# A graph layer with residual layer norm: GpSimd takes the first split of x, VectorE takes all the scaling, the first source columns are loaded directly, the short super is merged

## The reference

```python
x_i, x_j = x[dst], x[src]                       # x: 100000 x 48, f32
tmp = concatenate([x_i, x_j, edge_attr], 1)     # 25000 x 128
msg = relu(tmp @ W1 + b1) @ W2 + b2             # 25000 x 48
y = x + segment_sum(msg, dst, 100000)
out = (y - mean(y)) / sqrt(var(y) + 1e-5)       # per node, over 48 values
```

## Time and profile before

| | |
|---|---|
| runs | 394.97, 395.75, 395.84 us; median 395.75 |
| profiled execution | 395.34 us, its span 393.6 us |
| PE busy | 358.6 us, 91% |
| DVE busy | 369.7 us, 94% |
| ACT busy | 285.1 us, 72% |
| POOL busy | 281.6 us, 72% |
| gathers L877 | 196, mean 1084 ns |
| GpSimd's scales L886 | 72, mean 920 ns |
| queue q1 (SP) | 58.74 MB, 65.2% of 16 engines' span |

### The profile page before, as it was taken

One profiled execution on the slowest core, in us unless ns is written; L12 is line 12 of the kernel. 1 busy time (PEld: TensorE's weight loads), 2 busy tenths in 40 slices (PEclk: granted clock), 3 DMA queues, 4 the chain that ended last, 5 costly groups with the idle time before them and its releaser, 6 DMA issues.

```text
span 393.6 us, 18011 instructions
## 1 busy us (share of the span) xinstructions
PE 358.6 (91%) x6802; PEld 324.1 (82%) x6802; DVE 369.7 (94%) x1044; ACT 285.1 (72%) x791; POOL 281.6 (72%) x284
## 2 busy tenths in 40 slices
PE   3169999989999999999999999999999999999981
PEld 2047888878999999999998989998999999999971
DVE  6655999999999999999999999999999999999975
ACT  1046776776788787888787878878788878788861
POOL 6777777771688888888888888888888888212120
PEclk9999999999999999999999999999999999999995
DMA  4576889888878989989989989988988888753122
GB/s 87 103 152 129 134 182 212 182 180 206 181 160 178 185 180 183 198 181 201 206 166 231 200 173 198 218 186 177 231 181 176 199 191 164 174 152 98 49 81 78
DMA packets 165601, 66.38 MB, mean 169 GB/s; under 512 B 95213, under 2 KB 165554, under 8 KB 165554
## 3 DMA queue, kind: packets, MB, share of 16 engines
q1 hardware_dynamic: 152762, 58.74, 65.2%
q0 software_dynamic: 6272, 4.83, 9.7%
q10 hardware_dynamic: 6520, 2.26, 2.5%
HBM read 38.46 MB, written 27.33 MB: 167 GB/s over the span
## 4 chain that ended last, share of the span: by engine, by line
PE 66%; DVE 20%; POOL 4%; issue 4%; DMA 3%; ACTq 0%; SPq 0%; ACT 0%; DVEq 0%
PE bank L993 12%; PE bank L1013 11%; PE bank L1001 10%; PE bank L982 10%; PE bank L956 8%; PE bank L1020 8%; PE bank L950 6%; POOL rows L877 4%; DVE onehot L1262 3%; DVE sq_total L1280 3%; DVE ys L1238 3%; DVE total L1229 3%; DVE x_rest L1268 2%; DVE ys L1298 2%; DVE msg_rest L1245 1%
## 5 line engine op out<-in xcount | busy, mean ns | idle before, releaser
L877 POOL DMA_INDIRECT rows<-in_x_dram,src_cols x196 | 212.5, 1084 | 53.2 <-issue 50.4
L1082 ACT ACTIVATE onehot_t<-bank 128x384 bf16<-128x384 bf16 (+1 forms) x261 | 117.9, 491 | 18.4 <-PE bank L956 18.3
L1020 PEld LDWEIGHTS bank<-w,hid_t 128*128 128x128 f32 x522 | 95.5, 190 | 23.1
L886 POOL TENSOR_TENSOR ys<-ys,rstd 128x432 f32<-128x432 f32 x72 | 66.2, 920 | 46.3 <-DVE rstd L1288 45.2
L1020 PE MATMUL bank<-w,hid_t 128*128 128x48 f32 x522 | 82.5, 239 | 0.0
L956 PE MATMUL bank<-ident_b,onehot 128*128 128x128 bf16 (+1 forms) x782 | 73.1, 221 | 8.9 <-DVE onehot L1262 8.5
L1262 DVE TENSOR_SCALAR onehot<-node_of,cat 128x384 bf16<-128x384 f16 x260 | 69.0, 320 | 10.0 <-DMA cat<-edge_table 10.0
L1001 PE MATMUL bank<-cat_t,w 128*128 128x384 f32 (+1 forms) x176 | 71.3, 486 | 0.5 <-ACT cat_t L1070 0.5
L993 PE MATMUL bank<-msg,onehot 128*128 128x48 bf16 (+1 forms) x782 | 69.1, 184 | 2.2 <-DVE msg_low L1252 2.2
L1013 PEld LDWEIGHTS bank<-xs,onehot_t 128*128 128x128 bf16 (+1 forms) x782 | 69.2, 104 | 1.6 <-issue 0.9
L1013 PE MATMUL bank<-xs,onehot_t 128*128 128x48 bf16 (+1 forms) x782 | 69.6, 184 | 0.7 <-ACT onehot_t L1082 0.7
(11 more groups left out here) (109 smaller groups left out, 816.8 us busy)
## 6 DMA issues: line engine op xcount, KB each, us to landing
out_dram<-ys SPq DMA_DIRECT2D x43, 432.0 KB
xs<-in_x_dram SPq DMA_DIRECT2D x78, 216.0 KB
cat<-edge_table SPq DMA_DIRECT2D x261, 40.5 KB
edge_table<-rows SPq DMA_DIRECT2D x65, 121.5 KB
rows<-in_x_dram,src_cols POOLq DMA_INDIRECT x196
rows<-in_edge_attr_dram SPq DMA_DIRECT2D x28, 96.0 KB
xs<-in_x_dram ACTq DMA_DIRECT2D x8, 216.0 KB
rows<-in_edge_attr_dram ACTq DMA_DIRECT2D x1, 384.0 KB, 5.5
```

What stands on the lines that cost most here:

```text
L877: pool.indirect_dma_start(rows[:, t, 0:D], None, x[:, :], bass.IndirectOffsetOnAxis(ap=src_cols[:, t:t + 1], axis=0)).then_inc(xsrc_in[s], 16)
L886: pool.tensor_tensor(y, y, rstd[0:n, v, 0:m].unsqueeze(2).broadcast_to([n, m, D]), ALU.mult).then_inc(normed, 1)
L1020: last = pe.matmul(msg_ps[:, k * D:(k + 1) * D], hid_t[:, v % SMALL, k * P:(k + 1) * P], w2[:, :], start=False, stop=(k == blocks - 1))
L1082: act.activation(onehot_t[0:n, v % SMALL, k, 0:jj * P], onehot_ps[k % 2][0:n, 0:jj * P], ACT.Copy).then_inc(onehot_t_ready, 1)
```

## The change

GpSimd no longer scales. It makes x_rest for supers 10 on (RESTS_FIRST), in a loop that first issues the gathers for super g + 6, then waits for x of g and for the scale of super g - 6 (REST_BEHIND). VectorE makes x_rest for supers 0 to 9 and scales every super. Its list has another order: x_rest ahead of the message's split, the message's two splits next to each other, and x_low behind the onehots. The indices of the first three gathers are loaded as three columns of 128 by ScalarE's queue, ahead of its other loads. The 160 left nodes become the third block of super 86: 53 partitions of three nodes and one of one node. NS is 87, and the last super's x and output go in three transfers each. Its unused partitions hold what an earlier super left in the buffer.

```diff
-LEAD = 14
+LEAD = 6
+RESTS_FIRST = 10
+REST_BEHIND = 6
...
-FIRST_SCALED = 12
-LAST_SCALED = 4
+LAST_PARTS = 3
...
-    NS = FULL_SUPERS + 2
+    NS = NB // SUPER
...
         def wait_scaled(eng, g):
-            if FIRST_SCALED <= g < NS - LAST_SCALED:
-                eng.wait_ge(normed, g - FIRST_SCALED + 1)
-            else:
-                eng.wait_ge(dve_normed, g + 1 if g < FIRST_SCALED else g + 1 - (NS - LAST_SCALED - FIRST_SCALED))
+            eng.wait_ge(dve_normed, g + 1)
...
+        def last_rows(table, tile):
+            w, first, s = J * D, FULL * BLOCK, (NS - 1) % BODY
+            before, here = (SUPER - 1) * w, (NS - 1) * SUPER
+            return ((table[0:first, :].rearrange("(b p j) d -> p b (j d)", p=BP, j=J)[:, here:FULL, :],
+                     tile[:, s, 0:before].rearrange("p (b m) -> p b m", b=SUPER - 1)),
+                    (table[first:first + REST_P * J, :].rearrange("(p j) d -> p (j d)", j=J),
+                     tile[0:REST_P, s, before:before + w]),
+                    (table[first + REST_P * J:N, :].rearrange("(p j) d -> p (j d)", j=REST_J),
+                     tile[REST_P:REST_P + 1, s, before:before + REST_J * D]))
...
+                if g < NS - 1:
+                    sp.dma_start(sbuf_rows(xs, v), dram_rows(x, g)).then_inc(x_in[v], 16)
+                    return
+                for there, here in last_rows(x, xs):
+                    sp.dma_start(here, there).then_inc(x_in[v], 16)
...
+                if g == NS - 1:
+                    wait_scaled(sp, g)
+                    for there, here in last_rows(out, ys):
+                        sp.dma_start(there, here).then_inc(y_out[v // PAIR], 16)
+                elif g % PAIR == 0:
+                    wait_scaled(sp, g + PAIR - 1)
+                    sp.dma_start(dram_rows(out, g, PAIR), sbuf_rows(ys, v, PAIR)).then_inc(y_out[v // PAIR], 16)
...
+                if t == GROUP:
+                    pool.wait_ge(src_placed, 1)
+                cols = src_first if t < GROUP else src_cols
...
-            def scale(g):
-                n, blocks, jj = shape_of(g)
-                v, m = g % BODY, blocks * jj
-                pool.wait_ge(rstd_ready, g + 1)
-                y = by_node(ys, g, v)
-                pool.tensor_tensor(y, y, rstd[0:n, v, 0:m].unsqueeze(2).broadcast_to([n, m, D]),
-                                   ALU.mult).then_inc(normed, 1)
+            def less_high_x(g):
+                r, v = divmod(g, BODY)
+                pool.wait_ge(x_in[v], 16 * (r + (LAST_PARTS if g == NS - 1 else 1)))
+                pool.wait_ge(dve_normed, g - REST_BEHIND + 1)
+                pool.tensor_tensor(x_rest[:, v, :], xs[:, v, :], upper_half(xs[:, v, :]),
+                                   ALU.subtract).then_inc(pool_x_rest_ready, 1)
...
-            pool.wait_ge(src_placed, 1)
+            pool.wait_ge(src_first_in, 16 * GROUP)
...
-            for g in range(FIRST_SCALED, NS):
+            for g in range(RESTS_FIRST, NS):
                 for gathered in range(gathered, tiles_for(g + LEAD)):
                     gather_xsrc(gathered)
                 gathered = tiles_for(g + LEAD)
...
-                if g < NS - LAST_SCALED:
-                    scale(g)
+                less_high_x(g)
...
         def _(act):
+            for t in range(GROUP):
+                act.dma_start(src_first[:, t:t + 1], src[t * P:(t + 1) * P].rearrange("(p a) -> p a", a=1)).then_inc(src_first_in, 16)
             load_ends(act, 0, src, src_in)
...
             def less_high_x(g, r, v):
-                dve.wait_ge(x_in[v], 16 * (r + 1))
+                if g >= RESTS_FIRST:
+                    return
+                dve.wait_ge(x_in[v], 16 * (r + (LAST_PARTS if g == NS - 1 else 1)))
...
             def less_middle_x(g, r, v):
-                dve.wait_ge(x_rest_ready, g + 1)
+                if g < RESTS_FIRST:
+                    dve.wait_ge(x_rest_ready, g + 1)
+                else:
+                    dve.wait_ge(pool_x_rest_ready, g - RESTS_FIRST + 1)
...
-            walk(dve, ((4, total_sum), (5, total_squares), (4, centre), (3, less_high_msg), (0, less_high_x), (3, less_middle_msg),
-                       (0, less_middle_x), (-1, make_onehot), (5, invert), (5, scale_some), (0, flag_general)), looped=False)
+            walk(dve, ((4, total_sum), (5, total_squares), (4, centre), (0, less_high_x), (3, less_high_msg), (3, less_middle_msg),
+                       (-1, make_onehot), (0, less_middle_x), (5, invert), (5, scale), (0, flag_general)), looped=False)
```

More of the change, by code:

```diff
@@ L415, in gnn_resnorm_kernel @@
     NB = FULL + 1
-    RJ = 2
-    RP = REST // RJ
-    assert RP * RJ == REST and RP <= P and 0 < FULL % SUPER
+    REST_P = REST // J
+    REST_J = REST - REST_P * J
+    assert NB % SUPER == 0 and 0 < REST_P < P and 0 < REST_J < J
     FULL_SUPERS = FULL // SUPER
-    NS = FULL_SUPERS + 2
+    NS = NB // SUPER
     ROUNDS = (FULL_SUPERS - 3) // BODY
@@ L425, in gnn_resnorm_kernel @@
     EREST = E - EP * EC
-    assert NS % PAIR == 0 and BODY % PAIR == 0
+    assert NS % PAIR == 1 and BODY % PAIR == 0
     assert EP == P - 1 and 0 < EREST < EC
@@ L560, in gnn_resnorm_kernel @@
         src_in = sem("src_in")
+        src_first_in = sem("src_first_in")
         next_shifted = sem("next_shifted")
@@ L670, in wait_scaled, with sbuf_rows @@
         def wait_scaled(eng, g):
-            if FIRST_SCALED <= g < NS - LAST_SCALED:
-                eng.wait_ge(normed, g - FIRST_SCALED + 1)
-            else:
-                eng.wait_ge(dve_normed, g + 1 if g < FIRST_SCALED else g + 1 - (NS - LAST_SCALED - FIRST_SCALED))
+            eng.wait_ge(dve_normed, g + 1)
         def dram_rows(table, g, supers=1):
-            n, blocks, jj = shape_of(g)
[L680 to L691, removed]
+            return table[0:FULL * BLOCK, :].rearrange("(b p j) d -> p b (j d)", p=BP, j=J)[:, g * SUPER:(g + supers) * SUPER, :]
+        def sbuf_rows(tile, s, supers=1):
+            return tile[:, s:s + supers, :].rearrange("p s (b m) -> p (s b) m", b=SUPER)
+        def last_rows(table, tile):
[7 more added lines that the diff above has]
+                     tile[REST_P:REST_P + 1, s, before:before + REST_J * D]))
         def rows_in(g, r):
@@ L812, in load_nodes @@
                     sp.wait_ge(sum_done, g - BODY + 1)
-                sp.dma_start(sbuf_rows(xs, g, v), dram_rows(x, g)).then_inc(x_in[v], 16)
-            def store(g):
[L817 to L822, removed]
+                if g < NS - 1:
[3 more added lines that the diff above has]
+                    sp.dma_start(here, there).then_inc(x_in[v], 16)
+            def store(g):
+                v = g % BODY
+                if g == NS - 1:
[5 more added lines that the diff above has]
+                    sp.dma_start(dram_rows(out, g, PAIR), sbuf_rows(ys, v, PAIR)).then_inc(y_out[v // PAIR], 16)
             def nodes_behind(g):
@@ L1261, in make_onehot @@
                 for k in range(blocks):
-                    last = dve.tensor_scalar(onehot[:, v, k, 0:n * jj], nodes[:, 0:n * jj], float((first_block(g) + k) * BLOCK),
+                    last = dve.tensor_scalar(onehot[:, v, k, 0:n * jj], node_of[:, :], float((first_block(g) + k) * BLOCK),
                                              cat[:, v, k, P:P + 1], ALU.add, ALU.is_equal)
```

38 lines of the change are left out of this document (14 added, 24 removed).

## The result

The changed kernel takes 405.29 us, median of three runs (404.81 to 406.36), against 395.75 us before: ratio 1.0252, 95% interval 1.0228 to 1.0276. The profiled execution took 405.29 us with a span of 403.6. The direction was forecast, the size was not: +9.5 us where +3.3 was predicted.

The account below looks back on a forecast made before the run. VectorE bounds early steps, VectorE, TensorE and GpSimd run level in the middle (3.99 us), TensorE bounds the late ones. Span 40.1 + 23.4 + 310.8 + 22.7 = 397.0; time 395.75 + 3.3 = 399.0 us, range 391.5 to 413.

Parts of the forecast that it names:

- Floor: VectorE's new steady step: 4.47 less 0.52 for x_rest plus 0.12 for adjacent message splits, 4.07 us.
- Rival A: VectorE's adjacent message splits cost nothing: pace 3.96 us, not slower, 388.7 us; chance 0.12.
- Collisions: VectorE's delay beside GpSimd's work in the steady steps: 0.02 us a step, making the pace 4.09 (4.07 to 4.25).
- GpSimd's subtraction, 0.93 us: x_rest on GpSimd takes 0.93 us like its present scale (0.6 to 1.3), so GpSimd just keeps up.
- Rival B: GpSimd becomes the bound, 4.27 us a step if its subtraction takes 1.2 or gathers collide more: 412.9 us; chance 0.18.
- Part 2: GpSimd's new waits, with gathers and SP's transfers queued behind them, cost 0; without cover each missed step costs 4 us once.
- a sign of being wrong: VectorE or SP waiting for cat or for the edge table in the middle would show the forecast wrong.
- Steps 5 to 9, +0.6: VectorE keeps both jobs with the new adjacency: 5 x 0.12 = +0.6 us.
- Part 3: Three column loads first in ScalarE's queue let gathers start earlier: gain 1.2 us (-0.5 to 2.4).
- Part 4: Merged short super: shorter last steps -0.8 us, larger output in three pieces +1.0, tail +0.2.
- Rival C: No change: steady pace at 4.07 us with a favourable head start and tail, 395.5 us; chance 0.20.
- Rival D: The early column loads land late and bring nothing: 1.2 to 1.7 us above forecast, 400.5; chance counted within the forecast's 0.50.

Follow-up runs that it names:

- experiment 1: The changed kernel with the onehots put between the message split's two halves on VectorE: 392.54 us, ratio 0.9927 to the kernel before.
- experiment 3: The changed kernel with GpSimd waiting for the scale of super g-8 instead of g-6 (REST_BEHIND 8): 406.05 us.
- experiments 1 to 5: Five variants of the changed kernel; the fourth has the edits of experiment 1 and experiment 2 together: 399.08 us. The others have their own lines.
- Experiment 7: The kernel before with only the early source-column loads and the merged last super: 393.98 us, ratio 0.9966.
- experiment 6: The kernel before with only VectorE's list in the changed order, GpSimd still scaling: 396.20 us, ratio 1.0025.
- experiment 2: The changed kernel with 70 gathers issued ahead, then two each turn, and GpSimd's x_rest from super 16 instead of 10: 405.43 us.
- (5): The changed kernel with x_low ahead of the onehots again, the message split's halves still adjacent: 402.09 us, ratio 1.0176.

## Why the prediction was right and wrong, point by point

**Floor, "4.47 - 0.52 + 0.12 = 4.07 us": right,** to 0.01 in three steps of four. The 0.12 for the adjacency, read from the earlier trace rows against the earlier trace rows, is confirmed by taking it away (experiment 1). Rival A fell: an operation that waits for the one just ahead of it starts 0.12 us later, 0.33 to 0.34 against 0.21 to 0.22 for the same 128x144 subtraction. The Trainium skill (VectorE: DVE Perf Modes, The DRAIN you can't avoid) says the semaphore between chained operations costs nothing extra, which it measured on tensor_copy; for this pair of tensor_tensors the runs decide otherwise.

**Collisions, "I take 0.02, near the lower end because in three turns of four it is clear of msg_rest": wrong, and this is the step that failed.** Measured 4.17 - 4.07 = 0.10, five times as much: 0.082 x 76 = 6.2 of the 6.6 us by which the span came out over its forecast of 397.0. The mechanism of the floor was right; the term for collisions was mis-sized, though inside its own bounds of 0 to 0.18. Three turns of four are indeed clear. But the fourth costs 0.38, of which msg_rest's share (0.17) was in the forecast's bounds and the onehots' (0.21) in no term of its own. Sixteen such steps of 0.38 or 0.39 among the 76 make 6.1 us, 0.08 a step. Steps 39 and 43 (4.68 and 4.92) make another 1.5 us, 0.02 a step. In front of steps 42 and 43 a gather was issued late (GpSimd idle 1.55 us before the one at 197.71); why step 39 is long stays open.

I also had a row against my choice: the twelve early steps lost 0.08 each to GpSimd, with gathers alone beside them, and I let the reasoning about one operation overrule that. Those steps hold the very loss of the onehots that was missing from the sum, as shown above for step 10; I had read only step 9, one of the undisturbed ones.

**GpSimd's subtraction, 0.93 us: right,** 0.91, though with some luck, as it was taken from another operation. Rival B fell with it: GpSimd waits for VectorE, not VectorE for it. The room was larger than the 0.1 us that I gave it: between 100 and 340 us GpSimd waits 22.4 us for VectorE's scale, 0.39 a step. The 3.99 that I took for its need was the pace of all three engines, not its own work.

**Part 2, waits at cost 0: right.** VectorE never waits for cat in the middle, and loosening the wait (experiment 3) brings nothing. SP does wait for the edge table, 6 times and 1.9 us in all between 100 and 340 us. I had listed that as a sign of being wrong; it was a poor one, since no engine waits for cat because of it, and SP waited so in the kernel before too (18 times, 14.1 us in the whole run).

**Steps 5 to 9, +0.6: +0.9.** 0.12 each from the order; the rest is again onehots beside gathers.

**Part 3, -1.2: -0.6.** The three columns were issued from 0.8 to 1.8 us, 445 ns each, and landed 2.1 us later; the first gather starts at 4.12 instead of 5.85, inside the range of 3.4 to 5.9. Of these 1.7 us little reaches step 5. Its start lies between 39.67 and 40.99 in the profiled executions of the changed kernel and of experiments 1 to 5, which share that start-up, so a gain of one microsecond here is as large as its scatter. Experiment 7 has parts 3 and 4 together at 1.5 us.

**Part 4, +0.2: -0.3.** The last stores are issued 18.0 us after step 86 starts (399.42 less 381.45, before 18.4), and what follows takes 4.2 us (403.6 less 399.42, before 4.0). Two errors offset each other in part: the steps got 0.4 shorter, not 0.8, and the three pieces and six times the bytes cost 0.2, not the 1.0 that was charged. SP's timeline has the three issues in one line:

```profile
399.42 1.24 SPq L824 DMA_DIRECT2D out_dram<-ys  x3
```

**Rival C, no change, fell** with the collisions. Rival D, columns that land late, fell with the first gather at 4.12. The idea of the change was not at fault: with the messages apart it gives 392.54 us, against 393.98 with parts 3 and 4 alone. The place of one operation in the list costs the 12.75 us that turn this into a loss, the adjacency and the collisions together.

## What to carry to other kernels

When an engine takes on its last slack's worth of work, its list needs a second look: an operation right behind the one it waits for is free where the engine has slack and costs its delay in every step where it has none. A step's mean is its floor plus the rare long step; find out in which turn of the neighbour the long step comes, walk that whole turn and not only the operation that stalled before, and where a row already shows a loss per step, find the operation that has it before going by anything else. Check too that the operation that closes a ring between two engines stays early in the list.

## What the runs showed of the hardware that was not expected

**VectorE blocked by GpSimd ends at a fixed distance.** A VectorE subtraction caught by a subtraction or scale of GpSimd ends a set time after it, wherever it began. For the 128x144 message: before, GpSimd ends at 208.59 + 0.93 = 209.52 and msg_rest at 208.87 + 0.82 = 209.69; changed, 221.42 and 221.60; experiment 1, whose GpSimd subtraction ran from 213.22 for 0.91, 214.13 and 214.30. It is 0.17 or 0.18 each time, and 0.16 to 0.19 in all 136 msg_rests caught so after 60 us in ten of the traces. It holds even in step 61 of the kernel before, where msg_rest's recorded start is the earlier one: it runs from 272.76 for 1.36, to 274.12, and GpSimd's scale from 273.02 for 0.92, to 273.94. For the 128x432 x_rest of experiment 6 it is 0.47 (211.62 less 211.15), and 0.47 or 0.48 in all 14 cases. Both are the operation's own time less 0.13 (0.30 and 0.60 undisturbed), as if nearly all of it ran after GpSimd's end. Totals, squares' totals and centres beside it keep their 0.60. The Trainium skill (SBUF — State Buffer, SBUF: two separate sides) has VectorE operations with two SBUF inputs and GpSimd's reads exclude each other for a whole instruction; the 0.17 agrees. By it the stall can be worked out ahead: the end of GpSimd's operation + 0.17, less the end that msg_rest would have had. In the late turn that is 221.42 + 0.17 - 221.43 = 0.16, where 0.17 was measured.

**The onehots, too, can lose 0.21 us beside a gather,** 0.77 to 0.98 for three of 128x128, in the late turn's step. It goes when the late turn goes (experiment 2, in the middle) or when the onehots are moved (1), and can appear elsewhere (5). GpSimd's subtraction is not needed for it: the early steps of the kernel before have it with gathers alone. A gather is, as far as the twelve traces go: in steps 5 to 85 the onehots took more than 0.76 us to the next start in 118 of the 859 steps with a gather beside them, and in none of the 112 without. What picks the 118 stays open. The Trainium skill (SBUF — State Buffer, Who interferes with whom) says that a tensor_scalar can enter a 2-port mode and then contends with GpSimd, and that whichever of the two issues first holds the shared ports for its whole instruction. A loss on VectorE's side fits that; whether these tensor_scalars run in such a mode, no run here shows.
